# First layer's experts: a token list in packed order, made with one-hot products, in place of scattered rows

## The reference, cut to what matters

```python
scores = softmax(xf @ Wg); weights, indices = top_k(scores, 4)
C = 4 * T * 4 // 32                     # 2048 places
for e in range(32):
    pos = nonzero(pair_expert == e, size=C, fill_value=P)[0]
    tok = where(valid, pair_token[pos], 0); w = where(valid, pair_weight[pos], 0)
    y = y.at[tok].add((silu(xf[tok] @ W1[e]) * (xf[tok] @ W3[e])) @ W2[e] * w)
z = (silu(xf @ Ws1) * (xf @ Ws3)) @ Ws2
```

## Time and profile before

| | |
|---|---|
| median of three runs | 2562.9 us |
| the profiled execution's own time | 2555.89 us |
| its span | 2554.1 us |
| mean granted clock of TensorE | 0.942 |
| busy: PE, DVE, ACT, POOL | 2217.9, 1336.1, 785.3, 884.7 us |

### The profile page before, as it was taken

How to read it: one execution, slowest core, us unless ns; L and a number is a source line. 1 busy time by engine, 2 the same in 40 slices (tenths; PEclk the granted TensorE clock), 3 DMA queues, 4 the chain that set the end, 5 groups by cost and what they waited for, 6 DMA issues and landing times. The chain is left out here.

```text
span 2554.1 us, 40576 instructions
## 1 busy us (share of the span) xinstructions
PE 2217.9 (87%) x12182; PEld 1521.4 (60%) x12183; DVE 1336.1 (52%) x2971; ACT 785.3 (31%) x1695; POOL 884.7 (35%) x1090
## 2 busy tenths in 40 slices
PE   6999857767999576888888896999999999999997
PEld 3445534446999332333333333655579899998996
DVE  5553354344666475777677774479423333333332
ACT  2222312212333114655556664322211111111111
POOL 1100215667000536445543110122224444444443
PEclk9999977878999768999999999999999999999998
DMA  9997126224666535334542121310048888888885
GB/s 316 372 369 256 34 79 239 102 96 143 180 179 179 145 83 121 74 73 107 110 97 66 47 68 62 123 42 17 17 125 267 271 260 260 263 268 265 268 261 161
DMA packets 272711, 412.86 MB, mean 162 GB/s; under 512 B 32023, under 2 KB 226303, under 8 KB 272618
## 3 DMA queue, kind: packets, MB, share of 16 engines
q1 hardware_dynamic: 233962, 352.06, 42.5%
q0 software_dynamic: 38656, 59.70, 11.0%
HBM read 262.18 MB, written 148.89 MB: 161 GB/s over the span
## 5 line engine op out<-in xcount | busy, mean ns | idle before, releaser
L2659 PE MATMUL me_hp<-me_xgT,me_w 128*128 128x160 f32 x3072 | 436.6, 302 | 1.1 <-DVE me_xgT L2697 0.6
L2659 PEld LDWEIGHTS me_hp<-me_xgT,me_w 128*128 128x128 f32 x3072 | 421.4, 191 | 24.2 <-issue 22.8
L1393 DVE TENSOR_REDUCE hd_nmax<-hd_wide 128x2 f32<-128x1024 f32 x256 | 307.7, 1219 | 128.1 <-PE hd_wide L1131 125.0
L1322 ACT ACTIVATE hd_prob<-hd_slim 128x512 f32<-128x512 f32 x512 | 276.3, 602 | 191.2 <-PE hd_slim L1142 157.7
L2727 DVE TENSOR_TENSOR me_hid<-me_act_out,me_hp 128x160 f32<-128x160 f32 x384 | 123.3, 321 | 334.2 <-ACT me_act_out L2683 284.0
L2683 ACT ACTIVATE me_act_out<-me_hp 128x160 f32<-128x160 f32 x384 | 116.4, 303 | 558.6 <-PE me_hp L2659 467.1
L1142 PE MATMUL hd_slim<-hd_q_stack,hd_k_stack 100*128 100x512 bf16 x512 | 199.5, 393 | 39.9 <-ACT hd_prob L1322 33.5
L1131 PE MATMUL hd_wide<-hd_k_stack,hd_q_stack 97*128 97x512 bf16 x512 | 201.1, 397 | 32.2 <-DVE hd_rest L1387 15.9
L2028 PEld LDWEIGHTS mr_e_hp<-mr_e_xtT,mr_e_w_now 128*128 128x128 f32 x1280 | 169.3, 193 | 8.3 <-ACT mr_e_xtT L2048 0.2
L2028 PE MATMUL mr_e_hp<-mr_e_xtT,mr_e_w_now 128*128 128x128 f32 x1280 | 170.1, 276 | 0.0
L2314 PE MATMUL me_r_hp<-me_r_xnT,me_r_sw 128*128 128x512 f32 x384 | 167.5, 592 | 0.0
(11 more groups left out here) (384 smaller groups left out, 3607.0 us busy)
## 6 DMA issues: line engine op xcount, KB each, us to landing
me_w<-in_L_ffn_w_exp SPq DMA_DIRECT2D x192, 512.0 KB
places<-z_zero SPq DMA_DIRECT2D x64, 1152.0 KB, 11.1
me_w_first<-in_L_ffn_w_exp SPq DMA_DIRECT2D x32, 768.0 KB
me_w_second<-in_L_ffn_w_exp SPq DMA_DIRECT2D x32, 768.0 KB
mr_e_xt<-places SPq DMA_DIRECT2D x160, 144.0 KB, 2.3
outputs<-mr_e_y SPq DMA_DIRECT2D x160, 128.0 KB, 1.9
part_rows<-hd_parts SPq DMA_DIRECT2D x48, 256.0 KB
hd_k_stack<-part_rows SPq DMA_DIRECT2D x192, 64.0 KB
```

The lines of the kernel that those rows point to most:

```text
L1322: nc.scalar.activation(prob[:, u, :], slim[:, slim_slot(bt, item), :], ACT.Exp, scale=D ** -0.5)\
L1393: nc.vector.tensor_reduce(nmax[:, g % 2, n // 2, c:c + 2], wide[:, at], AX.X, ALU.max, negate=True)\
L2659: last = nc.tensor.matmul(hp[:, f % 3, half * CAP:(half + 1) * CAP], w1[:, sl, c, cols], xgT[:, sl, c, :], start=(c == 0), stop=(c == DC - 1))
```

## The change

The rows of all tokens go to DRAM once, in token order (routed_rows, one DMA of SP per batch, 589,824 bytes), and nothing is scattered. After the last batch DVE finds for each token its 4 packed rows (first row of the expert plus rank, plus one tile of 128, since tile 0 of outputs is now the tile of zeros for pairs over the capacity), split into tile and lane, in 4 groups of 8 token tiles. For each of the 32 token tiles POOL subtracts the lane from 0 to 127 (128 x 4 x 128), ACT squares it and takes max(0, number - number x square), which is the token's number where the lane is equal and 0 elsewhere; DVE makes the one-hot of the tile (128 x 4 x 160); and PE adds up the 4 products of the two in PSUM, 128 lanes x 160 tiles: the list of tokens. Three such pairs are in flight. Lanes without a token list token 0. POOL gathers the first 8 tiles by this list at the end of the block, and the other 152 in the second block, each when y of the tile 8 before is done; SP only stores there. The tensor place is written by DVE directly, and POOL's 65 instructions go. Of the clears one DMA of 128 KB stays, and the zero tile that POOL fills shrinks from 2,304 to 256 columns. The expert weights are loaded in four parts behind the row stores of the first four batches. The diff, cut (12 blanks of indent are left out where a line has as many):

```diff
-def mix_experts_routed(nc, ctx, x, ident, stats, mean, rstd, w_gate, w_in, w_out, places, outputs, scattered, place_out, earlier):
+def mix_experts_routed(nc, ctx, x, ident, stats, mean, rstd, w_gate, w_in, w_out, rows_out, outputs, place, earlier):
...
+        def gather(pool, n):
+nc.gpsimd.indirect_dma_start(out=xt[:, n % UNROLL, :], out_offset=None, in_=rows_out[:, :],
+                             in_offset=bass.IndirectOffsetOnAxis(ap=token[:, n:n + 1], axis=0)).then_inc(x_loaded[n % UNROLL], 16)
...
+SLOTS, ONES, GROUP = 4, 3, 2 * TB
+BIG = 65536.0
...
+        for b in range(B):
+            sp.wait_ge(rows_ready, b * TB + TB)
+            sp.wait_ge(gated, b + 1)
+            sp.dma_start(rows_out[b * S:(b + 1) * S, :].rearrange("(j p) n -> p j n", p=P), xg[:, b % SLOTS])\
+                .then_inc(stored[b % SLOTS], 16)
+            if b < B // 2:
+                es = slice(b * (2 * E // B), (b + 1) * (2 * E // B))
+                sp.dma_start(w1[:, es].rearrange("p e c n -> p e (c n)"), w_in[es].rearrange("e p n -> p e n")).then_inc(w_loaded, 16)
+                sp.dma_start(w2[:, es, :], w_out[es].rearrange("e p n -> p e n")).then_inc(w_loaded, 16)
+        for sem in stored:
+            sp.wait_ge(sem, 16 * (B // SLOTS))
+        sp.wait_ge(w_loaded, 16 * B)
...
+        pool.wait_ge(made, 7)
+        nc.gpsimd.tensor_scalar(less_number[:], number[:], -1.0, None, ALU.mult).then_inc(numbered, 1)
+        for t in range(NT):
+            pool.wait_ge(lanes_ready, t // GROUP + 1)
+            if t >= ONES:
+                pool.wait_ge(listed, t - ONES + 1)
+            nc.gpsimd.tensor_tensor(at_lane[:, t % ONES], lanes[:].unsqueeze(1).to_broadcast([P, TOP, P]),
+                                    lane_f[:, t, :].unsqueeze(2).to_broadcast([P, TOP, P]), ALU.subtract).then_inc(lane_off, 1)
+        for sem in stored:
+            pool.wait_ge(sem, 16 * (B // SLOTS))
+        pool.wait_ge(tokens_ready, 1)
+        for n in range(UNROLL):
+            gather(pool, n)
...
+        for t in range(NT):
+            pe.wait_ge(lane_numbered, t + 1)
+            pe.wait_ge(tile_made, t + 1)
+            for n in range(TOP):
+                last = nc.tensor.matmul(turned_list, at_lane[:, t % ONES, n, :], at_tile[:, t % ONES, n, :],
+                                        start=(t == 0 and n == 0), stop=(t == NT - 1 and n == TOP - 1))
+            last.then_inc(listed, 1)
+            if t == 2 * GROUP:
+                pe.wait_ge(tabled, 1)
+                for n in range(2):
+                    last = nc.tensor.transpose(tp[0:1, n * P:(n + 1) * P], table[:, n:n + 1], ident[:])
+                last.then_inc(table_turned, 1)
...
+        for t in range(NT):
+            act.wait_ge(lane_off, t + 1)
+            lane = at_lane[:, t % ONES].rearrange("p n l -> p (n l)")
+            nc.scalar.activation(lane, lane, ACT.Square).then_inc(lane_squared, 1)
+            act.wait_ge(lane_squared, t + 1)
+            act.wait_ge(numbered, 1)
+            nc.scalar.activation(lane, lane, ACT.Relu, bias=number[:, t:t + 1], scale=less_number[:, t:t + 1])\
+                .then_inc(lane_numbered, 1)
...
-                dve.wait_ge(scattered[b % SLOTS], 16 * TOP * TB * (b // SLOTS))
+                dve.wait_ge(stored[b % SLOTS], 16 * (b // SLOTS))
...
-        def placing(b):
+        def ranking(b):
 
             dve.wait_ge(rank_full, b + 1)
             chain.link(nc.vector.scalar_tensor_tensor(chosen[:], ranks, float(CAP), chosen[:], ALU.is_le, ALU.mult))
-            nc.vector.tensor_tensor(rank[:], ranks, first_place[:], ALU.add).then_inc(ranked, 1)
...
+            nc.vector.scalar_tensor_tensor(ranked_rows[:, b * TB:(b + 1) * TB, :], ranks, BIG, chosen[:], ALU.add, ALU.mult)\
+                .then_inc(ranked, 1)
+
+        def placing(g):
+
+            ts = slice(g * GROUP, (g + 1) * GROUP)
+            dve.wait_ge(ranked, (g + 1) * GROUP // TB)
+            rows_of = ranked_rows[:, ts, :]
+            chain.link(nc.vector.tensor_tensor(rows_of, rows_of, first_row[:].unsqueeze(1).to_broadcast([P, GROUP, E]), ALU.add))
+            for j in range(GROUP):
+                nc.vector.max(top_rows[:, j, :], ranked_rows[:, g * GROUP + j, :]).then_inc(top_done, 1)
+            dve.wait_ge(top_done, 2 * NT + (g + 1) * GROUP)
+            chain.link(nc.vector.tensor_scalar(row_f[:], top_rows[:, :, 0:TOP], BIG, BIG - (P - 1), ALU.max, ALU.subtract))
+            chain.link(nc.vector.tensor_copy(place[:, ts, :], row_f[:]))
+            chain.link(nc.vector.tensor_scalar(tile_i[:], place[:, ts, :], 7, None, ALU.arith_shift_right))
+            chain.link(nc.vector.tensor_copy(tile_f[:, ts, :], tile_i[:]))
+            nc.vector.scalar_tensor_tensor(lane_f[:, ts, :], tile_f[:, ts, :], -float(P), row_f[:], ALU.mult, ALU.add)\
+                .then_inc(lanes_ready, 1)
+            dve.wait_ge(lanes_ready, g + 1)
+
+        def tiles_of(t):
+
+            if t >= ONES:
+                dve.wait_ge(listed, t - ONES + 1)
+            nc.vector.tensor_tensor(at_tile[:, t % ONES], tile_nos[:].unsqueeze(1).to_broadcast([P, TOP, TILES]),
+                                    tile_f[:, t, :].unsqueeze(2).to_broadcast([P, TOP, TILES]), ALU.is_equal).then_inc(tile_made, 1)
...
+        def first_rows():
+
             dve.wait_ge(counted, 1)
             chain.link(nc.vector.tensor_scalar(count[:], counts, float(CAP), None, ALU.min))
...
+            chain.link(nc.vector.tensor_tensor(first_row[:], ends[:], tiles[:], ALU.subtract))
+            chain.link(nc.vector.tensor_scalar(first_row[:], first_row[:], float(P), None, ALU.mult))
...
-            placing(b)
+            ranking(b)
             if b + 2 < B:
                 rows(b + 2)
             hiddens(b)
-        table_of_tiles()
-        add(B - 1)
-        shifts()
+        first_rows()
+        for g in range(NT // GROUP):
+            placing(g)
+            if g == 1:
+                add(B - 1)
+                table_of_tiles()
+            for t in range(g * GROUP, (g + 1) * GROUP):
+                tiles_of(t)
         dve.wait_ge(table_turned, 1)
-        for dst, at in ((expert_y, LAG_S - LAG_Y), (tile_row, 2 * P + LAG_S)):
-            chain.tick(nc.vector.tensor_copy(dst[:], tp[0:1, at:at + dst.shape[1]]))
+        chain.tick(nc.vector.tensor_copy(expert_y[:], tp[0:1, 0:expert_y.shape[1]]))
+        dve.wait_ge(listed, NT)
+        nc.vector.tensor_copy(token[:], turned_list).then_inc(tokens_ready, 1)
         chain.wait()
         dve.wait_ge(y_free, B)
+        dve.wait_ge(tokens_ready, 1)
...
+        for n in range(UNROLL, TILES):
+            pool.wait_ge(y_ready, n - UNROLL + 1 + 2)
+            gather(pool, n)
...
 
         def store(n, u):
             sp.wait_ge(y_ready, n + 1 + 2)
...
+            sp.dma_start(outputs[bass.ds((n + 1) * P, P), :], y[:, u, :]).then_inc(y_stored[u], 16)
...
-    with sp.Fori(0, n_tiles // ROWS) as i:
-        sp.dma_start(places[bass.ds(i * (ROWS * P), ROWS * P), :].rearrange("(j p) d -> p j d", p=P), zero[:])\
-            .then_inc(cleared, 16)
-    sp.dma_start(outputs[last_tile:last_tile + P, :], zero[:, 0, 0:D]).then_inc(cleared, 16)
+    sp.dma_start(outputs[0:P, :], zero[:]).then_inc(cleared, 16)
...
```

More of the change, by code:

```diff
@@ L1783, in _ @@
                         second(b)
-                    pe.wait_ge(tabled, 1)
-                    for n in range(4):
-                        last = nc.tensor.transpose(tp[0:1, n * P:(n + 1) * P], table[:, n // 2, n % 2:n % 2 + 1], ident[:])
-                    last.then_inc(table_turned, 1)
+                    for t in range(NT):
[10 more added lines that the diff above has]
+                            last.then_inc(table_turned, 1)
                 @block.scalar
@@ L1882, in table_of_tiles @@
                     def table_of_tiles():
                         of_tile = [P, 2, E]
-                        dve.wait_ge(counted, 1)
-                        chain.link(nc.vector.tensor_scalar(count[:], counts, float(CAP), None, ALU.min))
-                        chain.link(nc.vector.tensor_tensor(over[:], count[:].unsqueeze(2).to_broadcast([P, E, PER]),
-                                                           steps_of[:].unsqueeze(1).to_broadcast([P, E, PER]), ALU.is_gt))
-                        chain.link(nc.vector.tensor_reduce(tiles[:], over[:], AX.X, ALU.add))
@@ L1900, in table_of_tiles @@
[L1900 to L1909 removed]
+                        chain.link(nc.vector.tensor_reduce(table[:], past[:], AX.X, ALU.add))
@@ L1947, in mix_experts_routed @@
             yp = k2.ps("yp", [P, 2, S])
-            x_loaded = [s.sem(f"x_loaded{j}") for j in range(UNROLL)]
             y_stored = [s.sem(f"y_stored{j}") for j in range(UNROLL)]
@@ L1983, in steps @@
                         for u in range(UNROLL):
-                            n = i * UNROLL + u
                             if not (first and u < LAG_S):
-                                store(n - LAG_S, (u - LAG_S) % UNROLL)
```

(9 more changed lines are left out.)

131 lines of the change are left out of this document (44 added, 87 removed).

## The result

The changed kernel takes **2591.8 us** in the median of four runs (2589.14 to 2597.46), the kernel before 2560.93 beside it (2553.03 to 2563.32): a ratio of 1.0129, 95% interval 1.01 to 1.0158. It is slower, by some 31 us, where 2554 was forecast.

| us | before | after | change |
|---|---|---|---|
| up to the first y | 599.2 | 587.0 | -12.2 |
| the tile loop, first to last y | 247.5 | 293.5 | +46.0 |
| from the last y to the end | 1707.4 | 1709.0 | +1.6 |

A forecast was written before the change was run, and what follows sets the result against it. The scatters were taken to bound the first part; counts 67 us sooner, less the new tail, put the first expert product 7.7 us sooner: 2555.9 - 7.7 = 2548.2, or 2555.2 from the median. Forecast 2554, range 2530 to 2592.

The forecast's parts named there:

- the tile loop at 1.557 us per tile: 160 tiles of the second block: PE-bound as before, one gather per tile at 1.26 us fits, so no cost.
- rival B: Tile loop: the steady stream of gathers holds signals between engines as the bursts did; +67 us, 2622; chance 0.11.
- Clears: 64 writes of zeros on SP's queue, under PE's attention: removal priced at nothing, bounds 0 to a few us gained.
- Rounds: First part's batches without scatters: 15.3 us each, counts used at 498.1 in place of 565.13, 67 us sooner.
- rival A: List tiles or rounds: POOL and DVE don't exclude each other, or rounds take 14.5; -22 us, 2535 to 2541; chance 0.30.
- List: Behind the last count: building the token list takes 76 us, 57.9 for 32 tiles and 6 at three borders.
- the sign that the prediction gave: List tiles: POOL's and DVE's tile instructions would never run at once, at a pitch of 1.8 to 2.1 us.
- Rival C: List tiles: ACT's squares and clamps need table loads between them, 1.28 us each, two per tile; +59 us; chance 0.04.
- Gathers and the change of blocks: After the list: copy 0.4 us, 8 gathers 10.1, next block 0.5 later, first product 1.7 after that, at 586.8.
- Late rows: Tile loop: a gather's rows land within 5.0 us of the 6.2 available, so hidden, with 1.2 us to spare.
- Rival D: Tile loop: DVE's copy, 0.41 us, adds to each gather, 1.67 per tile; net +9 us, 2571; chance 0.05.
- Rival E: First part: rounds aren't freed because signals were late for another cause; tail starts at 565, +59 us, 2621; chance 0.05.

The follow-up runs named there:

- e18: Changed kernel, loop in five streams: real gathers; then, with plain loads, gathers every second tile, 64-row gathers, plain POOL DMAs, POOL copies; 2562.60 us, ratio 0.9989.
- e14: The kernel before, unchanged, run as a control in the fourth set, in the free condition: 2514.64 us.
- e11: The changed kernel, unchanged, run as a control in the fourth set, in the free condition: 2538.72 us, ratio 1.0097 to the kernel before.
- e13: The changed kernel with empty lanes spread over 128 rows in place of all reading row 0, free condition: 2537.49 us, ratio 1.0088.
- e5: The kernel before, unchanged, run as a control for its trace, in the held condition: 2561.36 us, ratio 0.9979.

## Why the prediction was wrong

**The step that failed** is the tile loop at 1.557 us per tile, a term of nothing in the sum, and it rests on a sentence under rival B: "so the drain needs about 1.27 + 2/16 = 1.4 each (an estimate), and the loop issues one in 1.557". The loop took 1.846 per tile. I took the end of a burst's held signals for the end of its drain and let the whole rest of the burst drain at the pitch of issue. The runs show that a pitch of 1.54 is too fast: the loop held out for five gathers and then settled at 1.83 to 1.90 us per gather, while one per 3.1 us (e18's second stream) holds nothing. The rate that drains lies between these; 1.8 is where the loop settles, not a rate measured by itself. The row that could have warned was the same: a round of 24.5 us for 16 scatters is 1.53 each with the signals held in every round, and the loop was to issue at just that pitch. B had 0.11, with 75 us for the loop and +67 in all; it came with +46.0 in the loop, against -12.2 up to the first y. (Its 2622 is a slip: 75 on top of the forecast of 2554 is 2629.)

That 2591.8 lies within the stated 2530 to 2592 is luck: the high end had B at a third of its price, 25 us, and it came with nearly twice that, with a shorter first part to offset some of it.

The other steps:

- **Clears**, worth nothing: between 25 and 265 us PE is busy for 221.50 us, and for 221.23 in the kernel before.
- **Rounds** of 15.3 us and counts at 498.1: they came at 493.69, (479.6 - 381.2)/7 = 14.1 us a round, since L1899 waits 7.5 us in all in place of 39.5 and DVE's other remote waits, 21.0 us before, are gone. Right in mechanism, 4.4 us better; of rival A the faster rounds came (it had 14.5). Two small slips of the prediction do no harm: 9.7 + 3.6 + 1.3 is 14.6 and not 14.8, and 20.4 + 4.4 is 24.8, where the trace has 24.5 for a round of scatters, (583.2 - 388.8)/127 x 16. The counts come 71.4 us sooner than at 565.13.
- **List**, 76 us: 566.43 - 493.69 = 72.7. Inside it the exclusion of POOL and DVE was overstated. POOL's subtraction takes 1.04 us at 515.23 and 4.83/3 = 1.61 beside DVE's comparison, while 1.81 for a pair was forecast. ACT is as slow: 0.63 and 0.81 with a number per lane, 1.58 from one tile to the next, so POOL and ACT share the bound. POOL's and DVE's instructions did run at once, against the sign that the prediction gave. The borders make up the rest: POOL's groups of 8 begin 16.7 us apart (498.53, 515.23), where 8 x 1.81 + 2 = 16.5 was forecast; with 8 x 1.58 = 12.6 a border costs some 4 and not 2. Rival A's 43 us for the tiles didn't come.
- **Rival C**: no table load stands on ACT between 493 and 583 us, so square, clamp and the Silu before them went without one.
- **Gathers and the change of blocks**: 11.3 us from the list's copy to the end of the last gather (577.70), forecast with 10.5; but the next block began 3.7 later, at 581.39, and not 0.5. The 0.54 of the earlier trace rows is from a block end without indirect DMAs; what the 3.7 us are made of wasn't tested. First product at 582.60 in place of 586.8.
- **Late rows**, "1.2 to spare": PE waited 3.8 us in 160 tiles, and unread gathers cost as much as read ones. The term was right but for the last tiles.
- **Rival D**, which is theory C of the experiments: a gather takes 953 ns in the mean, and scatters and gathers before took 972 and 963; none pays a copy of 0.41. It is DVE's copies that grow, by 0.05 in the mean (421 to 471 ns), far less than the 0.29 that a tile lost.
- **Rival E** fell: the rounds were freed. In the free condition there was nothing to free.

By rival D's rule of the Trainium skill ("SBUF — State Buffer", the box on DVE blocking DMA in "SBUF: two separate sides") descriptor writing should wait for DVE's copy. No gather's length in these traces shows it: the one at 700.98 takes 0.98 us with a whole copy of DVE inside it (701.43 to 701.84). Whether the rule has a part in the late signals no run here tells; in e18 the same copies of DVE run beside POOL's plain DMAs at 1.58 per tile.

In the free condition the change loses as well, for another reason. From e14 to e11 the first y goes from 568.3 to 585.0 (+16.7), the loop from 247.7 to 254.7 (+7.0, most of it the empty tiles), the rest by +0.7 (1695.3 to 1696.0). The scatters follow each other at 1.276 us there, and the first part is over 30 us sooner; the counts are used at 493.1 in place of 506.0, 12.9 sooner, but behind them the list takes 70.2 us and its gathers 10 more, where the last scatter of e14 began 45.5 us behind its counts (551.5). The forecast's gain rested on held signals before and on none after.

## What to carry to other kernels

A transfer that is hidden by its duration can still cost through what its issue does to others: before moving indirect DMAs from a burst into a steady loop, compare the loop's pitch with the pitch of the burst that already held signals, not with the issue time of one. Run both kernels unchanged in every set of runs; the variants looked like cures here because the illness was absent. Where it comes and goes, put control and variants into stretches of one kernel and read the pitch of each from one trace.

## What the runs showed of the hardware

- In the held condition an indirect DMA for every tile of 1.55 us makes signals between PE, ACT and DVE late, ACT's by 2.3 us at 704.05, and the loop 1.83 to 1.90 us per tile, with 128 rows, 64 rows, or rows of 128 bytes alike; one for every second tile, or a plain DMA from POOL for every tile, doesn't (1.57 and 1.58), nor does POOL at work for 22 of 25 us.
- The same kernel took 2515 us in some sets of runs and 2560 in others, with scatters of 971 ns in both and the granted clock at 0.951 and 0.943 (e14, e5). The difference lies where indirect DMAs follow each other: 38.7 us up to the first y, where the scatters stand, and 15.0 behind the loop, where ACT waits 17.4 us beside the heads' gathers. The chip's number didn't decide it.
- In the free condition the gathers of the last tiles, taken to be those whose 128 lanes all read row 0, follow each other at 2.0 us; with the lanes spread over 128 rows at 1.54 (e11, e13).
